# Mixing the values right behind the scores in an attention step of a four-layer kernel

## What is computed

```python
kx = modulated_linear(x, s, k_aff_w, k_aff_b, k_w, k_b).reshape(B, N, H, D)   # H=16, D=32
q = k = v = kx
scores = einsum('bnhd,bnjd->bnhj', q, k) / sqrt(D)      # heads against heads, within one token
A = softmax(scores, axis=-1)
out = einsum('bnhj,bnjd->bnhd', A, v).reshape(B, N, F)
out = modulated_linear(out, s, o_aff_w, o_aff_b, o_w, o_b)
x = x + out
# layer 1: a low-rank linear layer whose weights come from the condition (rank 30)
# layer 2: modulated linear, clipped; layer 3: layer norms with gathered gains, then a two-layer MLP
```

## Time and profile before

| | |
|---|---|
| device time, 3 runs | 1090.22, 1092.92, 1093.40 us; median 1092.92 |
| the profiled execution | 1093.44 us, span 1091.6 us |
| PE | busy 1034.6 us, 95% of the span |
| POOL | busy 698.2 us, 64% |
| DVE | busy 663.5 us, 61% |
| ACT | busy 486.8 us, 45% |
| chain that ended last | PE 79%, issue 5%, POOL 5%, DVE 4%, ACT 3% |
| mean granted TensorE clock | 0.962 of full speed |

### The profile page before, as it was taken

The page is one execution under the profiler, slowest core; times in us unless marked ns, Lnnn a source line. Parts: engine busy times, 40 slices in busy tenths (PEclk is TensorE's granted clock), DMA queues, the critical chain, the costliest instruction groups (busy, mean ns, idle before and its releaser), DMA issues.

```text
span 1091.6 us, 18225 instructions
## 1 busy us (share of the span) xinstructions
PE 1034.6 (95%) x6598; PEld 804.6 (74%) x6598; DVE 663.5 (61%) x1209; ACT 486.8 (45%) x762; POOL 698.2 (64%) x636
## 2 busy tenths in 40 slices
PE   7898999989999998699999999999999999999993
PEld 5576777757766666478888888788888888888882
DVE  5467776667657665665656566666565656655441
ACT  2458777766547742343333234333333333333230
POOL 4345666566555543777877777777777777777852
PEclk9888999999889998899999999999999999999997
DMA  9262546444322245233233323413313314223210
GB/s 297 78 198 90 188 160 239 146 147 159 106 88 78 98 138 182 78 98 99 73 105 98 101 78 117 130 67 109 108 60 110 106 60 134 83 70 108 77 63 19
DMA packets 56012, 124.04 MB, mean 114 GB/s; under 512 B 7683, under 2 KB 9861, under 8 KB 54900
## 3 DMA queue, kind: packets, MB, share of 16 engines
q1 hardware_dynamic: 44148, 80.93, 21.8%
q0 software_dynamic: 11776, 41.95, 12.3%
HBM read 104.91 MB, written 17.95 MB: 113 GB/s over the span
## 4 chain that ended last, share of the span: by engine, by line
PE 79%; issue 5%; POOL 5%; DVE 4%; ACT 3%; SPq 2%; DMA 2%; POOLq 0%; DVEq 0%; ACTq 0%
PE ps L581 38%; PE ps_k L630 7%; PE ps_y L588 7%; PE ps_o L588 6%; PE tp L593 5%; PE ps_s L619 3%; PE ps_v L664 2%; PE tp L856 2%; PE ps L918 1%; PE ps_u L651 1%; PE ps_vt L611 1%; DMA x_in<-in_x_turned 1%; PE ps_s L616 1%; PE ps_t L675 1%; PE ps_x L97 1%
## 5 line engine op out<-in xcount | busy, mean ns | idle before, releaser
L1626 POOL TENSOR_TENSOR rstd<-var_eps,half 128x1 f32<-128x1 f32 x96 | 54.2, 565 | 131.0 <-DVE var_eps L1430 130.2
L1106 ACT ACTIVATE g_out<-ps 128x512 f32<-128x512 f32 x32 | 19.2, 599 | 178.1 <-PE ps L918 178.1
L935 ACT ACTIVATE at_diag<-at 32x512 f32<-32x512 f32 x128 | 80.3, 627 | 32.8 <-PE ps_v L664 23.9
L1555 POOL TENSOR_TENSOR om<-om,bc 128x512 f32<-128x512 f32 x32 | 44.1, 1378 | 74.8 <-DVE om L1247 74.8
L1571 POOL TENSOR_TENSOR e<-e,rinv 128x512 f32<-128x512 f32 x32 | 33.6, 1050 | 76.0 <-DVE rinv L1208 76.0
L935 ACT ACTIVATE k_diag<-kt 32x512 f32<-32x512 f32 x128 | 80.0, 625 | 1.1
L1436 DVE TENSOR_SCALAR shift_n<-mean_var,rstd 128x1 f32<-128x1 f32 x96 | 20.5, 214 | 94.6 <-POOL rstd L1626 92.5
L1057 ACT ACTIVATE h<-h,shift_n,rstd 128x512 f32<-128x512 f32 x32 | 26.1, 816 | 84.2 <-DVE shift_n L1436 84.2
L1416 DVE TENSOR_TENSOR t_lo<-tp,t_hi 128x512 fp32r<-128x512 f32 x64 | 43.8, 684 | 31.7 <-ACT t_hi L1053 31.7
L630 PE MATMUL ps_k<-wk_hi,xh 128*128 128x512 f32 x128 | 58.5, 457 | 0.1
L588 PE MATMUL ps_o<-oh,wo_hi 128*128 128x512 f32 x128 | 51.3, 401 | 4.3 <-DVE xb L1236 2.3
(11 more groups left out here) (271 smaller groups left out, 3281.7 us busy)
## 6 DMA issues: line engine op xcount, KB each, us to landing
raw<-in_dec_w SPq DMA_DIRECT2D x30, 512.0 KB, 5.9
x_in<-in_x_turned SPq DMA_DIRECT2D x32, 256.0 KB, 4.8
xb<-in_x_wide SPq DMA_DIRECT2D x32, 256.0 KB, 3.8
x_dram<-xb SPq DMA_DIRECT2D x32, 256.0 KB, 4.0
xt<-x_dram SPq DMA_DIRECT2D x8, 1024.0 KB, 8.2
out<-o SPq DMA_DIRECT2D x32, 256.0 KB, 2.0
raw<-in_int_W SPq DMA_DIRECT2D x7, 1024.0 KB, 6.2
wk_raw<-in_w_k_t SPq DMA_DIRECT2D x4, 256.0 KB, 4.2
```

The lines of the kernel that those rows point to most:

```text
L935: last = nc.scalar.activation(dst[g, :, q, :], src[g, :, :], ACT.Copy)
L1555: nc.gpsimd.tensor_tensor(om[:, :], om[:, :], bc[:, STYLE_O, t // TB, :], ALU.mult).then_inc(mix_step, 1)
L1626: nc.gpsimd.tensor_tensor(rstd[:, k:k + 1], var_eps[:, k:k + 1], half[:, :], ALU.pow).then_inc(norm_step[k], 1)
```

## The change

In PE's `attend`, the block of the mix moves from behind the `ps_u` product to right behind the scores. Its waits move with it. No instruction is added or removed, and the instructions of ACT, DVE, POOL and SP stand as before.

```diff
                         mm = nc.tensor.matmul(ps_s[D * g:D * g + D, Q * m:Q * m + Q, :], kt[p][:, j, :], k_diag[p][:, j, :, :],
                                               start=False, stop=True, skip_group_check=True)
                     mm.then_inc(scores_done, 1)
+                if has(3):
+                    t, p = s - 3, (s + 1) % 2
+                    pe.wait_ge(at_diag_ready, t + 1)
+                    pe.wait_ge(v_ready, t + 1)
+                    if later(t, 1):
+                        pe.wait_ge(mix_step, nth(MIX, "back", t))
+                    else:
+                        pe.wait_ge(style_bc_ready, B)
+                    for j in range(PR):
+                        m, q = divmod(j, Q)
+                        mm = nc.tensor.matmul(ps_v[D * q:D * q + D, Q * m:Q * m + Q, :, :], v[p][:, m, D * q:D * q + D], at_diag[:, j, :, :],
+                                              start=True, stop=True)
+                    mm.then_inc(mixed, 1)
                 if has(0):
                     pe.wait_ge(xl_ready, s + 1)
...
-                if has(3):
-                    t, p = s - 3, (s + 1) % 2
...
-                    mm.then_inc(mixed, 1)
                 if has(4):
                     t = s - 4
```

## The result

The changed kernel took 1084.07 us (median of 7 runs, 1080.05 to 1085.71), the kernel before beside it 1090.22 us (7 runs, 1089.29 to 1093.40). The ratio is 0.9923, 95% interval [0.9903, 0.9943]: faster by 6 to 11 us. The prediction said 1093.0, with 1088.5 to 1098.0 as its range. It was wrong. Of all executions behind this document, five took 1474 to 3509 us, some of them of the kernel before; they are in no median and no ratio.

What follows compares the result with a forecast made beforehand. PE, busy 95% of the span, was taken as the bound, gaining only through its waits. Terms 1.5 - 1.3 + 0.6 - 1.0 + 1.8 = +1.6 us, absorbed by the `xt` wait: 1093.0 us, range 1088.5 to 1098.

Steps and rivals of the forecast that it cites:

- PE's sum is unchanged if the mix finds its inputs ready: Regular steps: the same 1.08 us mix merely runs 5.6 us earlier; stall 0 to 0.1 us, taken as 0.
- PE's own order sets none of it: PE's 3.93 us wait on `xt`, ending at 423.26, hangs on other engines, so it takes up the 1.6 us loss.
- Steps 4 to 7, +1.5: Slow-clock steps: the mix waits for `at_diag`, 1.4 and 0.6 us, less 0.5 from `k_diag` waits; bounds 0 and 3.0.
- Step 20, -1.3: PE's 3.06 us wait for `u_row` shortens because `at_diag` comes earlier: -1.3 us, bounds 0 and -1.9.
- Steps 21 to 31, +0.6: Long DVE operations of `prepare` delay `mx` and `om`, giving one more stall: +0.6 us, bounds 0 and 2.
- Step 32, -1.0: No keys there; the mix fills PE's 1.98 us wait for `ol`: -1.0 us, bounds -0.9 and -1.9.
- the 1.7 that the prediction named and did not count: Step 32: a shorter hole may give back up to 1.7 us of the output product's slow clock; left out.
- Step 34, +1.8: The last mix waits for `at_diag`, no longer covered by the output product: +1.8 us, bounds 0 and 3.5.
- (a): Rival: the loop doesn't catch up, the mix waits for `om` in every short step; +3.3 to +7.2, about 1098 us; 17%.
- E: The end of the scores in a step, 128.72 in step 10; the next scores end at E + 9.16.
- (b): Rival: PE's waits hang on the ACT loop; half of 9.5 us (4.7) goes, giving 1088.7 us; 12%.
- (c): Rival: half clock in step 34 and one or two stalled steps; +1 to +3 after absorption, about 1095.5 us; 6%.

Runs made afterwards that it cites:

- the regular steps alone: Kernel before with the mix right behind the scores only in steps 8 to 31, the old place elsewhere: 1086.15 us, ratio 0.9945.
- the ends alone: Kernel before with the mix right behind the scores only in steps 3 to 7 and 32 to 34: 1091.68 us, ratio 1.0011.
- the old tail: Changed kernel with step 34 alone back in the old order (output product, mix, turn): 1086.06 us, 0.9943 of the kernel before.
- the second buffer: Kernel before with `at_diag` of odd tiles 3 to 15 in another buffer, cleared by GpSimd: 1086.27 us, ratio 0.9949.

## Why the prediction was wrong

**The step that failed first is "PE's sum is unchanged if the mix finds its inputs ready".** Its condition came true: there is no wait in steps 10 to 23 other than that for `u_row`, and the bounds of 0 to 0.1 us for the stall held. The conclusion was false. The same matmuls in another order took 0.28 us less in each step without the `ps_u` product, and 0.03 more in the others. With it fails the first sentence of the working, that PE's order pays only through time in which PE stands still. Of steps 8 to 31, 18 are of the first kind: 18 x -0.28 + 6 x 0.03 = -4.9 us; with the 1.5 us of waiting saved in step 20 that is -6.4, an estimate from the two traces, and the run of the regular steps alone gave -6.0. The 0 to 2 us by which the change measured more (6.9 and 8.4 by its two ratios) are not attributed; the slow step 21 that comes with the longer wait in part of the executions is the candidate that the traces show. One matmul put in between took most of it away again. It could have been read from the trace of before: the output matmuls follow each other in 0.23 us, the narrow block behind the last of them in 0.32. The prediction read durations of blocks (1.08 us for scores and mix alike) where the starts of neighbours were wanted.

**The second is "PE's own order sets none of it"**, of the wait on `xt`. The prediction held its end fixed at 423.26, so that whatever came before it, gain or loss, would be taken up. It ended at 413.14 in the changed kernel, and at 416.37 with the early mix in the regular steps alone, there with its full 3.9 us. SyncE's loads, which lead up to it, stand in SyncE's order behind the stores of `xb`, which the output products of the steps before lead to, and moved with them (407.74 to 399.34). A wait behind a pipeline is an anchor only if its releaser does not come out of that pipeline.

**Steps 4 to 7, +1.5.** The stalls came where they were forecast, steps 5 to 7, and larger (scores to mix 2.67, 2.11 and 2.67 us against 0.90). But the stretch did not get longer: 52.69 us against 54.00, and over all traces 52.7 to 54.3 with the mix right behind the scores and 50.3 to 54.1 with the old place. The stalls were real: PE stood still for 5.2 us of it, against 3.4 before (5.1 to 6.4 and 3.4 to 4.5 over the traces), 1.8 more. In these two traces the clock made up for it, 0.87 against 0.81. Over all traces it did not do so as a rule (0.84 to 0.87 against 0.81 to 0.90), and the means are 53.7 us with the early mix and 52.8 without. So the mechanism was right, the idle time near its forecast, and the cost in the end about 1 us, which is less than the traces of either order differ among themselves.

**Step 20, -1.3.** It gave -1.8: 1.5 by the wait, 0.3 by the borders. The mechanism and the size were right; the slow step 21 behind the longer wait, in three of five traces of the old order, had no term.

**Steps 21 to 31, +0.6.** One stall came, 1.5 us on `om` in step 24, yet that step took 14.08 us against 14.03. The term was of no consequence.

**Step 32, -1.0.** It gave -2.7. The hole was filled as described, and the output product behind it ran at full clock, 2.86 us against 4.54. That is the 1.7 that the prediction named and did not count, and it was right not to: in the four other traces with the old place in this step and the same wait of 2.0 to 2.1 us for `ol`, the product took 2.9 us and the step 9.7. Against those the early mix (8.5 to 8.7 us) gives -1.1, the forecast term. So what the prediction read off, that half clock follows a wait of this length, holds for that one execution and not for these four.

**Step 34, +1.8.** The place was right, the size not. The mix waited 2.35 us, for `om` and not for `at_diag`, and then mix and output product ran at half clock, 6.6 us from 386.47 to 393.05 where full clock takes 4.0. From the first transpose of step 33 to the L820 matmul ahead of the one that waits for `xt` it was 37.8 us instead of 31.5, +6.2, which besides these holds 0.9 of waiting for `at_diag` in step 33 and 1.1 for `fl` ahead of step 34; half of it came back in the shorter wait on `xt`, and the half clock behind that wait was gone too. The runs of the ends alone and of the old tail say that the whole is about zero.

**The rivals.** (a), the loop that does not catch up, did not occur, but it was close: `om` ends at 133.53 + 0.71 = 134.24, 0.15 us ahead of the next mix, which is E + 8.6 where the bounds were 8.7 and 9.2. Its price was put too low: from step 9 to 31 there are 17 steps without the product, not 14. (b) had the right direction and named what would be seen, PE at step 34 several us earlier and the wait on `xt` ending earlier, but its mechanism is not what the gain came from: freeing ACT in another way, with the second buffer, left the steps as long as they were (9.15 and 10.88 us), and PE's waits in the changed kernel are longer in sum, not shorter. What (b) is right about is the 1.5 us of step 20, which the second buffer did not reach. Its 1088.7 was reckoned from the profiled 1093.44; from the forecast of 1093.0 it is 1088.3, outside the stated range. Half clock in step 34 (c) came true and was paid back at `xt`.

## What to carry to other kernels

Where two orders of the same matmuls both keep PE fed, count how often PE passes between narrow and full-array weights; on this kernel, at 95% PE, that count made about 5 of the 6 to 8 us. Measure a block on PE from its start to the start of its neighbour, in both neighbourhoods. Before a wait is allowed to absorb anything, follow its releaser back to see whether it comes out of the loop that is being changed. And before a slow stretch in one trace is put down to the code, look for it in traces of kernels that have the same code there.

## What was unexpected of the hardware

Going from full-array matmuls to 32-column ones and back costs about 0.3 us: 0.32 against 0.23 us into the narrow block, 1.01 against 0.90 out of it, and then 0.49 against 0.43 to the next start for four transposes, or 0.34 against 0.23 for a 512-column matmul, as the first full-array block behind it.

GpSimd stood idle for 1.1 to 4.3 us in front of a gather in eleven traces, the gather starting 2.0 to 2.8 us behind an instruction packet each time. A few instructions more on that engine, far ahead, took packet and gap away: 0.30 us in all three kernels with such an addition.

The mean clock differs between executions of the same kernel, and the time with it: the kernel before took 1087.14 us at 0.970 and 1096.86 at 0.964 in one comparison. That is more than the whole effect of the change, so one pair of profiled executions (here 13 us apart, of which the change has 6 to 8) says where time goes but not how much.
